# Rotary keys from one product, with the halves swapped by DMA

## The chip, the cores and the metric

One Trainium2 chip; the program runs on one of its cores. The metric is the device time of one execution in microseconds (us); lower is better. The time given is a median over executions.

## What is computed

A cross attention block is followed by a routed feed forward block, for 8 batches of 512 tokens and 512 context rows, model width 1024. The part that the change touches is the rotary share of the attention scores:

```
kv_c   = kv @ W_kvc                          # 512 x 256
k_rope = _rope(kv_c @ W_kr)                  # 512 x 64, one for all 16 heads
q_rope = _rope((q_c @ W_qr) per head)        # 512 x 64 per head
_rope(x) = [x1*cos - x2*sin, x1*sin + x2*cos]   # x1, x2: halves of 32
scores = (q_nope . k_nope + q_rope . k_rope) / sqrt(192)
```

## The kernel before, in words

Each engine has its own program, written out by hand; semaphores join them. In every product each float32 operand is split into a high part (fp32r) and a low part (the rest), and three of the four cross products are summed: high by high, high by low, low by high. ScalarE (ACT) makes the high part from the PSUM bank, VectorE (DVE) or GpSimd (POOL) the low part. The split weights are written to DRAM in the first batch and reloaded in the later ones. SyncE (SP) issues nearly all DMAs, one after another in a fixed order, and a wait on that queue holds all that stand behind it.

A batch is one run through 16 heads in 4 quads of 4. Each head has 4 score tiles of 128 queries by 512 keys (`scores`, five products of 512 columns into psS: k_hi by q_hi, k_hi by q_lo, the rotary stack by k_rope_hi and by k_rope_lo, k_lo by q_hi). Between them TensorE (PE) makes the next head's queries (`queries`, 9 products into psA) and keys (`keys`, 6 into psB), the values, the turned probabilities, the attention output and the output projection.

Between two batches (`body`, end, and `into_heads`) PE does the down projections of queries and context, then `rope_keys`, `queries(b, 0, 0)`, `keys(b, 0, 0)`, the last piece of the last batch's output projection (`out_end`, only when there was a batch before), and the first score tile. `rope_keys` (L1837) is 12 products: 6 with W_kr into psA and 6 with W_kr whose column halves are exchanged and signed into psB, each with its 64 columns written twice so that all 128 partitions are filled. VectorE's `rope_k` (L1250) multiplies psA by the cosines into `rope_term`, psB by the sines into `k_rope_term`, and adds them (L1261). ScalarE's `k_rope_hi` (L1020) and GpSimd's `k_rope_lo` (L746) make the two parts `krh` and `krl`, which the first score tile waits for.

The rotary queries of a quad are made by `rope_q`, and SP spreads them over the stack (`stack_head`, L469): per head four DMAs of 32 partitions by 512 elements. In the first batch all four heads' are issued in a row (`into`, L502), later only the first head's before the feed forward's loads (`ffn_loads`), the others behind.

## Time and profile before

| | |
|---|---|
| median of 3 executions | 3238.69 us (3235.26 to 3240.01) |
| the profiled execution's own time | 3238.15 us |
| its span in the trace | 3236.4 us |
| TensorE matmul busy | 3069.6 us, 95% of the span |
| VectorE busy | 2083.3 us, 64% |
| ScalarE busy | 1490.6 us, 46% |
| GpSimd busy | 714.7 us, 22% |
| mean granted TensorE clock | 0.977 |

Times in the trace are microseconds from the start of the span; a batch takes some 381 of them, and 1.75 us of the profiled execution lie outside the span. A row of the timeline gives an instruction's start and its duration; the start of the next one on the engine, not the duration, tells how fast a run of them goes. "Idle" in brackets is the time for which the engine had nothing, and what ended it.

### The profile page before, as it was taken

Reading aid. Unit: us, or ns where it says so; the run is one execution under the profiler, and the core shown is the slowest. Engines: PE = TensorE matmul, PEld = TensorE weight load, DVE = VectorE, ACT = ScalarE, POOL = GpSimd, SP = SyncE. Lnnn points to the kernel's source line nnn. Section 1 sums busy time; section 2 is a strip of 40 time slices with the busy share of each in tenths; the row PEclk is TensorE's granted clock in tenths of the full one; section 3 lists DMA queues with packets and bytes.
Section 4 is the critical chain, followed back from the end, with each engine's and each line's share of the span. In section 5 each row is a group of like instructions: output and inputs, shape, how many; then the busy total and the mean of one; then the engine's idle time right before and its main releaser. Section 6 shows DMA issues by size and latency. Waiting matters only on the chain.

```text
span 3236.4 us, 39942 instructions
## 1 busy us (share of the span) xinstructions
PE 3069.6 (95%) x13890; PEld 2386.5 (74%) x13890; DVE 2083.3 (64%) x4440; ACT 1490.6 (46%) x2907; POOL 714.7 (22%) x516
## 2 busy tenths in 40 slices
PE   7999999999999999999999999999999999999924
PEld 4788768887788867888678876888678876888722
DVE  2555537775577746777377764777467763777687
ACT  2655525553445435445264543555345452555411
POOL 5222241112211131110411113111311113111046
PEclk9999999999999999999999999999999999999955
DMA  6554444444534445433454444444454444544301
GB/s 205 195 172 160 173 163 164 136 140 148 192 121 140 140 156 189 134 128 130 156 193 140 140 146 172 141 140 140 141 181 140 140 131 150 186 140 137 118 27 4
DMA packets 170054, 473.34 MB, mean 146 GB/s; under 512 B 33136, under 2 KB 61424, under 8 KB 149248
## 3 DMA queue, kind: packets, MB, share of 16 engines
q1 hardware_dynamic: 164784, 469.91, 43.7%
q0 software_dynamic: 5072, 0.88, 0.6%
q8 instruction: 114, 1.87, 0.2%
q14 instruction: 84, 0.69, 0.1%
HBM read 369.84 MB, written 67.31 MB: 135 GB/s over the span
## 4 chain that ended last, share of the span: by engine, by line
PE 83%; DVE 7%; issue 4%; ACT 3%; POOL 2%; DMA 1%; SPq 0%; DVEq 0%; ACTq 0%; POOLq 0%
PE psC L1934 18%; PE psD L1927 10%; PE psA L1864 8%; PE psT L1916 6%; PE psA L1833 5%; PE psB L1873 5%; PE psD L1884 4%; PE psS L1901 3%; PE psB L1833 3%; PE psS L1907 3%; PE psS L1903 3%; PE psS L1902 3%; PE psS L1904 3%; PE psA L1855 2%; PE psB L1855 2%
## 5 line engine op out<-in xcount | busy, mean ns | idle before, releaser
L1934 PE MATMUL psC<-w_o_pair,attn_hi 128*128 128x512 f32 x1920 | 638.4, 413 | 18.7 <-DVE acc L1342 10.8
L1033 ACT ACTIVATE exps_ring<-exps_ring,neg_max 128x512 f32<-128x512 f32 x512 | 370.8, 724 | 424.9 <-DVE neg_max L1314 424.9
L1314 DVE CUSTOM_DVE_ANT_0 exps_ring<-psS,mask 128x512 f32<-128x512 f32 x512 | 353.2, 690 | 294.4 <-PE psS L1907 289.1
L1044 ACT ACTIVATE probsT_hi<-psT 128x512 fp32r<-128x512 f32 x512 | 305.8, 599 | 364.9 <-PE psT L1916 363.3
L1934 PEld LDWEIGHTS psC<-w_o_pair,attn_hi 128*128 128x128 f32 x1920 | 332.2, 189 | 89.5 <-DVE acc L1342 24.9
L1039 ACT ACTIVATE exps_ring<-exps_ring,row_sum_inverse 128x512 f32<-128x512 f32 x512 | 369.6, 722 | 61.0 <-DVE row_sum_inverse L1320 61.0
L1326 DVE TENSOR_TENSOR probsT_lo<-psT,probsT_hi 128x512 fp32r<-128x512 f32 x512 | 350.6, 686 | 58.3 <-ACT probsT_hi L1044 56.6
L1934 PE MATMUL psC<-w_o_pair,attn_lo 128*128 128x512 f32 x960 | 379.4, 395 | 0.0
L1342 DVE TENSOR_TENSOR acc<-acc,psC 128x512 f32<-128x512 f32 x448 | 303.2, 677 | 17.3 <-PE psC L1934 11.4
L1916 PE MATMUL psT<-ident,exps_ring 128*128 128x128 f32 x2048 | 305.0, 272 | 0.0
L1916 PEld LDWEIGHTS psT<-ident,exps_ring 128*128 128x128 f32 x2048 | 252.8, 139 | 66.4 <-issue 2.1
L1864 PE MATMUL psA<-q_c_hi,w_uq_ring 128*128 128x512 f32 x768 | 258.5, 391 | 0.1
L1934 PEld LDWEIGHTS psC<-w_o_pair,attn_lo 128*128 128x128 f32 x960 | 180.7, 188 | 42.2
L1901 PE MATMUL psS<-k_hi,q_hi 128*128 128x512 f32 x512 | 203.2, 397 | 6.0 <-DVE q_lo L1291 4.9
L1907 PE MATMUL psS<-k_lo,q_hi 128*128 128x512 f32 x512 | 200.4, 391 | 0.0
L1903 PE MATMUL psS<-k_rope_hi,q_rope_stack 128*128 128x512 f32 x512 | 199.7, 390 | 0.0
L1902 PE MATMUL psS<-k_hi,q_lo 128*128 128x512 f32 x512 | 199.7, 390 | 0.0
L1927 PE MATMUL psD<-probsT_hi,values_lo 128*128 128x512 f32 x512 | 199.5, 390 | 0.0
L1904 PE MATMUL psS<-k_rope_lo,q_rope_stack 128*128 128x512 f32 x512 | 199.4, 390 | 0.0
L1927 PE MATMUL psD<-probsT_hi,values_hi 128*128 128x512 f32 x512 | 199.2, 389 | 0.0
L1927 PE MATMUL psD<-probsT_lo,values_hi 128*128 128x512 f32 x512 | 199.2, 389 | 0.0
L1873 PE MATMUL psB<-kv_c_hi,w_uk_ring 128*128 128x512 f32 x512 | 180.3, 393 | 0.0
(301 smaller groups left out, 5497.8 us busy)
## 6 DMA issues: line engine op xcount, KB each, us to landing
w_o_pair<-w_o_split SPq DMA_DIRECT2D x112, 1024.0 KB, 5.4
w_uq_ring<-w_uq_split SPq DMA_DIRECT2D x114, 384.0 KB, 3.5
w_uv_quad<-w_uv_split SPq DMA_DIRECT2D x29, 1024.0 KB, 5.0
w_uk_ring<-w_uk_split SPq DMA_DIRECT2D x114, 256.0 KB, 2.8
w_qr_sorted<-w_qr_split SPq DMA_DIRECT2D x29, 768.0 KB, 4.3
x_stage<-in_x_dram SPq DMA_DIRECT2D x32, 512.0 KB, 5.9
x_stage<-in_ctx_dram SPq DMA_DIRECT2D x32, 512.0 KB, 4.1
acc<-in_x_dram SPq DMA_DIRECT2D x32, 512.0 KB, 5.3
```

What stands on the lines that cost most here:

```text
L1033: act.activation(E[:, qt, :], E[:, qt, :], ACT.Exp, scale=-1.0, bias=mx[:, i % 2, qt:qt + 1], accum_out=rs[:, i % 2, qt:qt + 1]).then_inc( ...
L1039: act.activation(E[:, qt, :], E[:, qt, :], ACT.Copy, scale=ri[:, i % 2, qt:qt + 1]).then_inc(s_prob, 1)
L1044: act.activation(PT[0][:, :, qt * P:(qt + 1) * P], psT[qt % 2][:, :].rearrange("p (c n) -> p c n", c=TT), ACT.Copy)\
L1314: dve.tensor_tensor_reduce(E[:, qt, :], psS[qt % 2][:, :], mask[:, qt, :], -SCALE, BIG, ALU.add, ALU.min, mx[:, i % 2, qt:qt + 1]).then_in ...
L1326: dve.tensor_tensor(PT[1][:, :, qt * P:(qt + 1) * P], psT[qt % 2][:, :].rearrange("p (c n) -> p c n", c=TT), hi.bitcast(F32), ALU.subtract ...
L1342: dve.tensor_tensor(a, a, psC[:, :], ALU.add).then_inc(freeC, 1)
L1864: mm_ = pe.matmul(psA[:, :], wuq[:, i % 2, s, c, :], qc[a][:, c, :], start=c + s + a == 0, stop=c == QB - 1 and s == 1)
L1873: mm_ = pe.matmul(psB[:, :], wuk[:, i % 2, s, c, :], kvc[a][:, c, :], start=c + s + a == 0, stop=c == CB - 1 and s == 1)
L1901: pe.matmul(ps, qh[:, cols], kh[:, :], start=True, stop=False)
L1916: mm_ = pe.transpose(psT[qt % 2][:, c * P:(c + 1) * P], E[:, qt, c * P:(c + 1) * P], ident)
L1927: mm_ = pe.matmul(psD[:, :], V[v][:, kt, i * P:(i + 1) * P], PT[p][:, kt, :], start=kt == 0 and v + p == 0, stop=kt == TT - 1 and v == 1)
L1934: mm_ = pe.matmul(ps[:, :], attn[a][:, 2 * pair + i, t * P:(t + 1) * P], WO[:, half, o, i, :], start=i + a + o == 0, stop=i + a == 2)
```

## The change

It touches one stage, between the down projection of the context and the first score tile of a batch, and the setup of W_kr:

- W_kr's columns are laid out once as 128: the 64 plain ones, then the 64 exchanged and signed ones. `rope_keys` is 6 products into psB alone; A0, the first position in psA's count, goes from 4 to 3.
- VectorE multiplies partitions 0 to 63 of psB by the cosines and 64 to 127 by the sines, both into `rope_term`. SP copies each half of it to the other half of `k_rope_term` (two DMAs, new function `swap_halves`, new semaphore), and VectorE adds the two. The sum stands behind `q_lo`.
- On ScalarE the high part of the first queries now stands ahead of `k_rope_hi`, that of the first keys behind it as before.
- In every score tile k_lo by q_hi is now third and the two rotary products last; in the first tile of a batch the waits for `krh` and `krl` stand directly before them.
- In SP's order `swap_halves` stands behind all four heads' stack loads in the first batch, and behind the first head's in the others, ahead of the feed forward's loads.
- The split W_kr that is stored and reloaded is half as large.

```diff
+            def swap_halves(b):
+                sp.wait_ge(freeB, b * BN + 4)
+                sp.dma_start(rk[0:R, :], rt[R:P, :]).then_inc(s_swap, 16)
+                sp.dma_start(rk[R:P, :], rt[0:R, :]).then_inc(s_swap, 16)
+
             def into(b, q, nxt, between=None):
...
                 if b == 0:
                     for i in range(HQ):
                         stack_head(b, q, i)
+                    if q == 0:
+                        swap_halves(b)
                     return
                 load_qr(b, q, nxt)
                 stack_head(b, q, 0)
+                if q == 0:
+                    swap_halves(b)
                 ffn_loads(b, q)
                 if between is not None:
                     between()
...
             def kr_hi():
-                act.wait_ge(s_setv, 4)
-                for w in range(2):
-                    act.activation(wkrs[:, w, 0], wkrr[:, w], ACT.Copy).then_inc(s_seta, 1)
+                act.wait_ge(s_setv, 2)
+                act.activation(wkrs[:, 0], wkrr, ACT.Copy).then_inc(s_seta, 1)
 
...
                 down(psB, fullB, b * BN + 2, kvc[0][:, 0, :], s_kvchi)
                 down(psA, fullA, b * AN + 3, kvc[0][:, 1, :], s_kvchi)
+                q_hi(b, 0, 0)
                 k_rope_hi(b)
-                q_hi(b, 0, 0)
                 k_hi(b, 0, 0)
...
-            def rope_k(b):
+            def rope_k_terms(b):
 
                 dve.wait_ge(s_rope, b * NR + 4)
                 dve.wait_ge(s_rhi, b * (NQ + 1) + 1)
                 dve.wait_ge(s_rlo, b * (NQ + 1) + 1)
-                dve.wait_ge(fullA, b * AN + 5)
-                dve.tensor_tensor(rt[:, :], psA[:, :], cosT[:, :], ALU.mult).then_inc(freeA, 1)
                 dve.wait_ge(fullB, b * BN + 4)
-                dve.tensor_tensor(rk[:, :], psB[:, :], sinT[:, :], ALU.mult).then_inc(freeB, 1)
-                dve.wait_ge(freeA, b * AN + 5)
+                dve.tensor_tensor(rt[0:R, :], psB[0:R, :], cosT[0:R, :], ALU.mult)
+                dve.tensor_tensor(rt[R:P, :], psB[R:P, :], sinT[R:P, :], ALU.mult).then_inc(freeB, 1)
+
+            def rope_k_sum(b):
                 dve.wait_ge(freeB, b * BN + 4)
+                dve.wait_ge(s_swap, 32 * (b + 1))
                 dve.tensor_tensor(rt[:, :], rt[:, :], rk[:, :], ALU.add).then_inc(s_rope, 1)
 
             def rope_q(b, q):
@@ -1456,8 +1466,9 @@
                 kvc_lo(b, 1, psA, freeA)
                 if ends is not None:
...
-                rope_k(b)
+                rope_k_terms(b)
                 q_lo(b, 0, 0)
+                rope_k_sum(b)
                 k_lo(b, 0, 0)
...
-            for a in range(2):
-                dve.tensor_copy(wkrr[:, 0, :, a, :], wkr).then_inc(s_setv, 1)
-            for a in range(2):
-                dve.tensor_scalar(wkrr[:, 1, :, a, 0:HR], wkr[:, :, HR:R], -1.0, None, ALU.mult)
-                ins = dve.tensor_copy(wkrr[:, 1, :, a, HR:R], wkr[:, :, 0:HR])
-            ins.then_inc(s_setv, 1)
-            for w in range(2):
-                dve.wait_ge(s_seta, 2 + w)
-                dve.tensor_tensor(wkrs[:, w, 1], wkrr[:, w], wkrs[:, w, 0].bitcast(F32), ALU.subtract)\
-                   .then_inc(s_wkrd, 8)
+            dve.tensor_copy(wkrr[:, :, 0, :], wkr)
+            dve.tensor_scalar(wkrr[:, :, 1, 0:HR], wkr[:, :, HR:R], -1.0, None, ALU.mult)
+            dve.tensor_copy(wkrr[:, :, 1, HR:R], wkr[:, :, 0:HR]).then_inc(s_setv, 1)
+            dve.wait_ge(s_seta, 2)
+            dve.tensor_tensor(wkrs[:, 1], wkrr, wkrs[:, 0].bitcast(F32), ALU.subtract).then_inc(s_wkrd, 16)
...
             def rope_keys(b):
                 pe.wait_ge(s_wkrd, 16 * (b + 1))
-                for ps, full, free, n, w in ((psA, fullA, freeA, b * AN + 4, 0),
-                                             (psB, fullB, freeB, b * BN + 3, 1)):
-                    wait_free(free, n)
-                    for c in range(CB):
-                        for s, a in ((0, 0), (0, 1), (1, 0)):
-                            mm_ = pe.matmul(ps[:, :], wkrs[:, w, s, c].rearrange("p a r -> p (a r)"), kvc[a][:, c, :],
-                                            start=c + s + a == 0, stop=c == CB - 1 and s == 1)
-                    mm_.then_inc(full, 1)
+                for c in range(CB):
+                    for s, a in ((0, 0), (0, 1), (1, 0)):
+                        mm_ = pe.matmul(psB[:, :], wkrs[:, s, c].rearrange("p w r -> p (w r)"), kvc[a][:, c, :],
+                                        start=c + s + a == 0, stop=c == CB - 1 and s == 1)
+                mm_.then_inc(fullB, 1)
 
             def rope_queries(b, q):
...
-                    if i == 0 and q == 0:
-                        pe.wait_ge(s_rhi, b * (NQ + 1) + 2)
-                        pe.wait_ge(s_rlo, b * (NQ + 1) + 2)
                 if not (very_first and qt < 2):
                     pe.wait_ge(s_sm, n - 1)
                 cols = slice(qt * P, (qt + 1) * P)
                 ps = psS[qt % 2][:, :]
                 pe.matmul(ps, qh[:, cols], kh[:, :], start=True, stop=False)
                 pe.matmul(ps, ql[:, cols], kh[:, :], start=False, stop=False)
-                pe.matmul(ps, stack[:, i, cols], krh[:, :], start=False, stop=False)
-                pe.matmul(ps, stack[:, i, cols], krl[:, :], start=False, stop=False)
                 if qt == 0:
                     pe.wait_ge(freeB, pos_b(b, q, 1 + i) + 1)
-                pe.matmul(ps, qh[:, cols], kl[:, :], start=False, stop=True).then_inc(s_S, 1)
+                pe.matmul(ps, qh[:, cols], kl[:, :], start=False, stop=False)
+                if qt == 0 and i == 0 and q == 0:
+                    pe.wait_ge(s_rhi, b * (NQ + 1) + 2)
+                pe.matmul(ps, stack[:, i, cols], krh[:, :], start=False, stop=False)
+                if qt == 0 and i == 0 and q == 0:
+                    pe.wait_ge(s_rlo, b * (NQ + 1) + 2)
+                pe.matmul(ps, stack[:, i, cols], krl[:, :], start=False, stop=True).then_inc(s_S, 1)
 
             def turn_probs(b, q, i, qt):
 
```

On the SP queue, in the first batch: the last stack loads and what follows them. Before:

```order
34 L479 DMA q_rope_stack<-rope_out 32x512 x2
35 L479 DMA q_rope_stack<-rope_hi 32x512 [waits rope_lo_done,rope_hi_done]
36 L479 DMA q_rope_stack<-rope_hi 32x512
37 L479 DMA q_rope_stack<-rope_out 32x512 x2
38 L373 DMA xT<-in_L_xattn_W_uq_dram 128x3x128 [waits fullB,fullA]
39 L377 DMA xT<-in_L_xattn_W_uk_dram 128x2x128
```

and with the change:

```order
34 L480 DMA q_rope_stack<-rope_out 32x512 x2
35 L480 DMA q_rope_stack<-rope_hi 32x512 [waits rope_lo_done,rope_hi_done]
36 L480 DMA q_rope_stack<-rope_hi 32x512
37 L480 DMA q_rope_stack<-rope_out 32x512 x2
38 L505 DMA k_rope_term<-rope_term 64x512 [waits freeB]
39 L506 DMA k_rope_term<-rope_term 64x512
40 L374 DMA xT<-in_L_xattn_W_uq_dram 128x3x128 [waits fullB,fullA]
41 L378 DMA xT<-in_L_xattn_W_uk_dram 128x2x128
```

The two copies stand behind the sixteen stack loads (four for each of four heads) and ahead of the raw weights of the coming heads.

VectorE at the same place, from the low part of the context to the first score tile's mask (`kv_c_lo` is the low part of the down projection). Before:

```order
39 L1247 TENSOR_TENSOR kv_c_lo<-psA,kv_c_hi 128x512 [waits kv_c_hi_done]
40 L1256 TENSOR_TENSOR rope_term<-psA,cosT 128x512 [waits rope_lo_done,fullA,rope_hi_done,rope_steps]
41 L1258 TENSOR_TENSOR k_rope_term<-psB,sinT 128x512 [waits fullB]
42 L1261 TENSOR_TENSOR rope_term<-rope_term,k_rope_term 128x512 [waits freeB,freeA]
43 L1291 TENSOR_TENSOR q_lo<-psA,q_hi 128x512 [waits q_hi_done]
44 L1296 TENSOR_TENSOR k_lo<-psB,k_hi 128x512 [waits k_hi_done]
45 L1314 ISA exps_ring,neg_max<-psS,mask 128x512 [waits scores,mask_steps]
```

and with the change:

```order
36 L1256 TENSOR_TENSOR kv_c_lo<-psA,kv_c_hi 128x512 [waits kv_c_hi_done]
37 L1265 TENSOR_TENSOR rope_term<-psB,cosT 64x512 [waits rope_lo_done,fullB,rope_hi_done,rope_steps]
38 L1266 TENSOR_TENSOR rope_term<-psB,sinT 64x512
39 L1301 TENSOR_TENSOR q_lo<-psA,q_hi 128x512 [waits q_hi_done]
40 L1271 TENSOR_TENSOR rope_term<-rope_term,k_rope_term 128x512 [waits k_rope_halves_swapped,freeB]
41 L1306 TENSOR_TENSOR k_lo<-psB,k_hi 128x512 [waits k_hi_done]
42 L1324 ISA exps_ring,neg_max<-psS,mask 128x512 [waits scores,mask_steps]
```

The sum has moved behind `q_lo` and waits for the copies; `k_lo` stands behind the sum.

ScalarE at the same place, before:

```order
24 L959 ACTIVATE kv_c_hi<-psB 128x512 [waits fullB]
25 L959 ACTIVATE kv_c_hi<-psA 128x512 [waits fullA]
26 L1022 ACTIVATE k_rope_hi<-rope_term 128x512 [waits rope_steps]
27 L1008 ACTIVATE q_hi<-psA 128x512 [waits fullA]
28 L1012 ACTIVATE k_hi<-psB 128x512 [waits fullB]
```

and with the change:

```order
23 L969 ACTIVATE kv_c_hi<-psB 128x512 [waits fullB]
24 L969 ACTIVATE kv_c_hi<-psA 128x512 [waits fullA]
25 L1017 ACTIVATE q_hi<-psA 128x512 [waits fullA]
26 L1031 ACTIVATE k_rope_hi<-rope_term 128x512 [waits rope_steps]
27 L1021 ACTIVATE k_hi<-psB 128x512 [waits fullB]
```

`q_hi` has moved ahead of `k_rope_hi`; `k_hi` still stands behind it.

## Rows read from the trace of the kernel before

**Rows 1.** The page: the span, and TensorE's busy time and instructions.

```profile
span 3236.4 us, 39942 instructions
...
PE 3069.6 (95%) x13890; PEld 2386.5 (74%) x13890; DVE 2083.3 (64%) x4440; ACT 1490.6 (46%) x2907; POOL 714.7 (22%) x516
```

**Rows 2.** The timeline of PE at the last change of batches: start, duration, instruction.

```profile
2745.79 0.47 PE L1844 MATMUL psA<-kv_c_hi,w_kr 128*128 128x512 f32 x1
...
2753.35 0.39 PE L1901 MATMUL psS<-k_hi,q_hi 128*128 128x512 f32 x1
...
2754.48 0.39 PE L1864 MATMUL psA<-q_c_hi,w_uq_ring 128*128 128x512 f32 x1
```

**Rows 3.** The timeline of DVE at the same place.

```profile
2747.53 0.69 DVE L1256 TENSOR_TENSOR rope_term<-psA,cosT 128x512 f32<-128x512 f32 x1 [1.15 <-PE psA L1844]
...
2749.58 0.69 DVE L1261 TENSOR_TENSOR rope_term<-rope_term,k_rope_term 128x512 f32<-128x512 f32 x1
2751.46 0.69 DVE L1291 TENSOR_TENSOR q_lo<-psA,q_hi 128x512 fp32r<-128x512 f32 x1 [1.18 <-ACT q_hi L1008]
...
2756.48 1.27 DVE L1359 BATCH_NORM_STATS2 ffn_stats<-xT 128x6 f32<-128x512 f32 x2
```

**Rows 4.** The timeline of ACT at the same place.

```profile
2750.31 0.63 ACT L1022 ACTIVATE k_rope_hi<-rope_term 128x512 fp32r<-128x512 f32 x1 [5.39 <-DVE rope_term L1261]
2750.85 0.58 ACT L1008 ACTIVATE q_hi<-psA 128x512 fp32r<-128x512 f32 x1
```

**Rows 5.** The timeline of POOL at the same place.

```profile
2751.02 1.29 POOL L748 TENSOR_TENSOR k_rope_lo<-rope_term,k_rope_hi 128x512 fp32r<-128x512 f32 x1 [17.72 <-ACT k_rope_hi L1022]
```

**Rows 6.** The timeline of SP's queue at the same place: the feed forward's first load.

```profile
2744.31 0.35 SPq L490 DMA_DIRECT2D xT<-out_dram  x1
```

**Rows 7.** Line L479 from 73 to 84 us: sixteen stack loads.

```profile
DMA to landing us min/median/max: 2.0/2.0/3.4
```

**Rows 8.** Line L490, all of its seven loads.

```profile
DMA to landing us min/median/max: 3.6/3.6/3.7
```

**Rows 9.** The timeline of DVE, second head: two operations back to back.

```profile
2764.78 0.69 DVE L1291 TENSOR_TENSOR q_lo<-psA,q_hi 128x512 fp32r<-128x512 f32 x1
2765.39 0.68 DVE L1296 TENSOR_TENSOR k_lo<-psB,k_hi 128x512 fp32r<-128x512 f32 x1
```

**Rows 10.** The timeline of PE, second head of the last batch.

```profile
2765.52 0.50 PE L1901 MATMUL psS<-k_hi,q_hi 128*128 128x512 f32 x1 [0.41 <-DVE q_lo L1291]
```

**Rows 11.** The timeline of SP's queue in the first batch.

```profile
82.57 1.23 SPq L479 DMA_DIRECT2D q_rope_stack<-rope_out  x2
83.89 0.53 SPq L373 DMA_DIRECT2D xT<-in_L_xattn_W_uq_dram  x1
```

**Rows 12.** The timeline of PE in the first batch.

```profile
70.86 0.47 PE L1844 MATMUL psA<-kv_c_hi,w_kr 128*128 128x512 f32 x1 [1.51 <-DVE kv_c_lo L1247]
...
79.62 0.40 PE L1864 MATMUL psA<-q_c_hi,w_uq_ring 128*128 128x512 f32 x1
...
91.66 0.50 PE L1901 MATMUL psS<-k_hi,q_hi 128*128 128x512 f32 x1 [1.40 <-DVE q_lo L1291]
```

**Rows 13.** The timeline of ACT in the first batch.

```profile
86.67 0.52 ACT L968 ACTIVATE w_uq_ring<-xT 128x384 fp32r<-128x384 f32 x1 [2.11 <-DMA xT<-in_L_xattn_W_uq_dram]
```

**Rows 14.** The timeline of PE: its two longest waits between the batches and near the end.

```profile
400.38 1.61 PE L1822 MATMUL psS<-ident,x_stage 128*128 128x128 f32 x8 [3.42 <-DVE x_stage L1238]
...
3083.78 1.22 PE L1934 MATMUL psC<-w_o_pair,attn_hi 128*128 128x512 f32 x2 [2.48 <-DVE acc L1627]
```

**Rows 15.** Windows: stretch, busy us of PE, PEld, DVE, ACT, POOL; granted clock; DMA share; GB/s.

```profile
70.80:74.00 3.20, 3.02 (x13) 2.24 (x13) 0.81 (x2) 0.00 (x0) 2.13 (x1) 1.00 0.00 0
401.00:404.00 3.00, 3.00 (x11) 2.52 (x10) 0.00 (x0) 1.19 (x2) 0.00 (x0) 0.50 0.88 296
3083.80:3087.00 3.20, 3.20 (x8) 2.52 (x9) 3.16 (x4) 0.00 (x0) 0.00 (x0) 0.50 0.00 0
```

**Rows 16.** Windows: the first batch from its first score tiles to its end.

```profile
80.00:445.00 365.00, 355.13 (x1645) 281.04 (x1644) 198.92 (x427) 200.51 (x394) 115.09 (x82) 1.00 0.51 172
```

More of the change, by code:

```diff
@@ L42, in xattn_ffn_kernel @@
     assert T == HALF and HQ * HR == P and 2 * R == P and D == 2 * HALF and NT * SLICE == D
-    A0, AQ = 4, 1 + HQ
+    A0, AQ = 3, 1 + HQ
     B0, BQ = 3, 1 + HQ
@@ L111, in xattn_ffn_kernel @@
             wDkv = sb_under("w_kvc", [P, DB, KVC])
-            wkrs = sb_under("w_kr", [P, 2, 2, CB, 2, R], F32R)
+            wkrs = sb_under("w_kr", [P, 2, CB, 2, R], F32R)
             rk = sb_under("k_rope_term", [P, T])
@@ L190, in xattn_ffn_kernel @@
         gb_end = xs[:, 1, :]
-        wkrt = wkrs[:, :, :, :, :, :].rearrange("p w s c a r -> p (w s c a r)")
+        wkrt = wkrs[:, :, :, :, :].rearrange("p s c w r -> p (s c w r)")
         wkr = acc[:, 1, 0:CB * R].rearrange("p (c r) -> p c r", c=CB)
-        wkrr = acc[:, 1, HALF:HALF + 4 * CB * R].rearrange("p (w c a r) -> p w c a r", w=2, c=CB, a=2)
+        wkrr = acc[:, 1, HALF:HALF + 2 * CB * R].rearrange("p (c w r) -> p c w r", c=CB, w=2)
         uq_raw0 = E[:, 0:2, 0:QB * P].rearrange("p s (c n) -> p s c n", c=QB)
@@ L238, in xattn_ffn_kernel @@
         s_krs = sem("w_kr_out")
+        s_swap = sem("k_rope_halves_swapped")
         s_gam = sem("gamma_in")
@@ L297, in xattn_ffn_kernel @@
         wo_dram = nc.dram_tensor("w_o_split", [PAIRS, 2, P, 4 * HALF], F32).ap()
-        kr_dram = nc.dram_tensor("w_kr_split", [P, 8 * CB * R], F32).ap()
+        kr_dram = nc.dram_tensor("w_kr_split", [P, 4 * CB * R], F32).ap()
         ss_dram = nc.dram_tensor("slope_sign_scratch", [NT, SLICE], F32).ap()
```

## The prediction

> **What bounds the kernel now.** I read the page first: TensorE is busy for 3069.6 us of a span of 3236.4 [rows 1], so the time is TensorE's order of work plus its waits. Then the timeline of the place that the change touches, in the last batch. TensorE starts the first rotary key product at 2745.79, the first score tile at 2753.35 and the work behind that tile at 2754.48, with no wait between [rows 2]: 33 products in 7.56 us, 0.229 each, and 5 more in 1.13 us. I call 2745.79 zero; the tile begins at 7.56 and the next work at 8.69. The other engines do the rotary keys beside this and are done in time: the sum of the terms starts at 2749.58 [rows 3], its high part at 2750.31 [rows 4], its low part at 2751.02 with 1.29 us [rows 5], ready at 2752.31, a microsecond before the tile. So the products are what costs time here, and the chain behind them is covered by 21 products. The change takes away 6 products and lengthens that chain by a trip through the DMA queue. The question is which of the two ends last.
>
> **Removed: 6 products in each of 8 batches.** 6 x 0.229 = 1.37 us a batch, 11.0 in all, if nothing else is late. TensorE would then reach the first tile at 6.19. VectorE has one bank less to read, and the first queries no longer wait for VectorE to free psA.
>
> **Added: the chain through the copies, batches 2 to 8.** Step by step from zero:
> - The 6 products into psB end where those into psA end now, so the first term starts at 1.74, as L1256 does at 2747.53 [rows 3].
> - Two operations on 64 partitions each. I take 0.69 us each, that of 128 partitions, since the elements per partition are the same. The second starts 0.61 after the first if it goes as two independent ones do now (2764.78 and 2765.39 [rows 9]), or up to 0.73 later if it waits for its end. I take 0.67; the terms are done at 3.10. The Trainium skill, "VectorE: DVE Perf Modes", section "Two Vector instructions with no wait between them", says that an instruction which starts in another quarter of the partitions than the one ahead starts only when all earlier ones have finished. That speaks for 0.73 here, and by it the sum below would be 0.5 us higher over 8 batches; no row here shows such a pair.
> - SP is idle then: it issued the feed forward's first load at 2744.31 [rows 6], and that one now stands behind the copies. It issues the first copy 0.03 later, at 3.13, and the second 0.61 behind it, as two stack loads take 1.23 us [rows 11]: 3.74.
> - Landing. No row has a copy of 64 partitions between the two halves. Nearest are the stack loads, 32 partitions each: 2.0 us in the median, 3.4 at most [rows 7]. Nothing in a copy excludes 2.0, and nothing is shorter in those rows. I take 2.2, a little over the quiet one because it carries twice the bytes and the loads that were under way here now come later. It lands at 5.94, and the sum starts at 5.97.
> - From the sum's start: the high part 0.73 later (2749.58 to 2750.31), the next operation of ScalarE 0.54 behind it [rows 4], which is k_hi now, since k_hi stands behind k_rope_hi; VectorE's low part starts 0.61 after it (2750.85 to 2751.46 [rows 3]) and takes 0.69; TensorE takes it 0.05 later (q_lo ends at 2765.47, the product starts at 2765.52 [rows 9, 10]). That is 2.62, so k_lo by q_hi starts at 8.59. Three products of 0.227 follow, and the next work starts at 9.27.
> - The low part of the rotary keys on GpSimd is ready 0.73 + 0.71 + 1.29 = 2.73 after the sum's start [rows 3 to 5]; its product comes at 3.07. It costs nothing; its cover is k_lo and two products, 0.34 us.
>
> Against 8.69 before, that is **+0.58 us a batch**, 4.1 for seven. The saved 1.37 us are spent as a wait of about 1.7 us before the tile, and what was expected to be hidden is not, above all because k_hi, needed by the tile's first product, queues behind the rotary high part on ScalarE. Moving the rotary products last does not help when the first product waits for the same chain. Break even is a landing of 1.6 us.
>
> **The first batch.** SP issues sixteen stack loads in a row there; the last two start at 82.57 and the next DMA at 83.89 [rows 11]. The copies stand behind them, while their terms have long been ready. First copy 83.89, second 84.50, landed 86.70, sum 86.73, next work behind the tile 3.30 later: 90.03. Before it was 79.62 [rows 12]: **+10.4 us**. Two corrections. TensorE waits for 1.40 us at 91.66 [rows 12], where the second head of the last batch waits for 0.41 [rows 10]; the excess comes from ScalarE, which stood until 86.67 for raw weights [rows 13]. With everything else ten microseconds later these weights are in time: -1.0. And TensorE is idle for more than 12 us (from about 76 to 88.7). After idle times of 3.42 and 2.48 us [rows 14] the granted clock was 0.50, the lower of the two levels, 1.2 GHz, in the stretches 401 to 404 and 3083.8 to 3087 [rows 15]. 3.2 us at half clock lose 1.6 us of work: +1.6, up to twice that. First batch: **+11.0**.
>
> **What is moved.** The feed forward's first two loads start at 2744.31 now [rows 6] and would start at about 4.4 after zero, 2750.2; 3.6 us [rows 8] make 2753.8, and VectorE uses the first at 2756.48 [rows 3]. Hidden by 2.7 us. Without that cover each microsecond would hold VectorE ahead of the second tile's mask. The two extra issues, 1.2 us, also push back the raw weights of the first batch; they are hidden by the ten microseconds above. The stack loads of the later heads stand behind the last store of the batch as before.
>
> **The order in every tile.** k_lo by q_hi is third, so k_lo must be there two products after the tile's start. In the second head k_lo ends at 2766.07 [rows 9] and the tile starts at 2765.52 [rows 10]; the product after a wait takes 0.50 instead of 0.39, so the third is due at about 2766.09. I take 0.03 us for two such heads a batch, 0.5 in all, between 0 and 0.14 each. Other tiles have the same five products: 0. The shorter setup of W_kr and its smaller reload lie beside long down projections: 0.
>
> **Sum.** 4.1 + 11.0 + 0.5 = +15.6 us on the profiled execution's 3238.15: **3253.8 us**. The median of the runs is 3238.69, so the profiled execution stands for them.
>
> **Rivals.**
> - *The clock falls in the later batches too.* The wait before the tile, 1.7 us and another 0.2 before the third product, lies between an idle time of 1.51 us, after which the clock was 1.00 [rows 12, 15], and one of 2.48, after which it was 0.50 [rows 14, 15]. If it falls each time, 1.6 us are lost seven times: +11.2, **3265 us**. The Trainium skill, "TensorE: Matmul & The Clock Gate", part 1, calls the lower clock the default that activity lifts; the two falls above agree, and by that rule alone this rival could come true in some batches and not in others. Chance 0.15.
> - *The copies land late.* At 3.1 to 3.4 us, as some stack loads do [rows 7], each batch loses 0.9 to 1.2 more, 8 to 9 in all: **3262 us**. Against it: no load is under way at this point any more. Chance 0.13.
> - *The first batch absorbs its delay.* The mechanism: the waits of that batch are set by chains of DMAs and split weights on SP and GpSimd that do not pass through the delayed tile. TensorE is idle for 9.9 of the 365 us from 80 to 445 [rows 16], 3.42 of them at 400.38 [rows 14]. If all of that were such, 1.1 of 11.0 us would be left, and the time would be 3238.15 + 1.1 + 4.6 = **3243.9 us**, no change within 0.2%. It decides from 9.1 us absorbed. Against it: SP's loads in that batch wait for TensorE's progress head by head. Chance 0.05.
> - *The saving comes through.* Only if the copies land 0.2 us after their issue, a tenth of the shortest stack load, would all 1.37 us be saved in seven batches, 9.6, against 9.5 in the first and its order: **3238 us**. Chance 0.02.
>
> **How the numbers follow.** The forecast's own case has 0.65. With a landing of 2.0 us, the pair at 0.61, half the clock's loss and no cost of the order it gives 3238.15 + 7 x 0.32 + 10.0 = 3250.4; with a landing of 2.5 and a clock loss of 3.2 it gives 3257.8. The range reaches to late copies and to the clock falling in every batch on one side, and below the own case on the other for a part absorbed: 3247 to 3266. 0.2% of the time, 6.5 us, is about what a measurement of this kernel can tell from no change, so the bound is 3245.2 on the median. Slower: 0.65 + 0.15 + 0.13 = 0.93, less a little, 0.92; within the bound: 0.06; faster: 0.02.
>
> **What would show it.** In the trace after: 6 products fewer a batch; in batches 2 to 8 a wait of 1.5 to 1.9 us before the first tile, released by k_hi, and the copies landing 2.0 to 2.5 us after their issue; the work behind the first tile 9.1 to 9.5 us after the first rotary key product. In the first batch a wait of 12 to 13 us that ends near 89 us, with a granted clock of 0.50 behind it, and everything later shifted by some 11 us. It is wrong if the copies land so early that no wait stands before the tile, or if the time from the first batch's end to the last one's is not longer than before.

## The result, and the profile after

| | before | after |
|---|---|---|
| median | 3237.57 us (3235.26 to 3240.01, 4 runs) | 3256.61 us (3254.73 to 3258.33, 4 runs) |
| the profiled execution, its span | 3238.15, 3236.4 us | 3256.62, 3254.5 us |
| TensorE matmul busy | 3069.6 us | 3066.2 us |
| mean granted TensorE clock | 0.977 | 0.975 |

The ratio is 1.0059, with a 95% interval from 1.0041 to 1.0076: slower. The medians lie 19.0 us apart, the profiled executions 18.5, and 15.6 were forecast. The page has 48 products fewer than [rows 1], six a batch:

```profile
span 3254.5 us, 39840 instructions
...
PE 3066.2 (94%) x13842; PEld 2373.1 (73%) x13842; DVE 2080.7 (64%) x4436; ACT 1491.9 (46%) x2906; POOL 715.4 (22%) x516
```

The timeline of PE, last batch, which answers to [rows 2]. The first rotary key product is zero again:

```profile
2764.46 0.50 PE L1847 MATMUL psB<-kv_c_hi,w_kr 128*128 128x512 f32 x1
...
2772.54 0.47 PE L1901 MATMUL psS<-k_hi,q_hi 128*128 128x512 f32 x1 [1.67 <-issue]
...
2773.22 0.50 PE L1905 MATMUL psS<-k_lo,q_hi 128*128 128x512 f32 x1
...
2774.03 0.40 PE L1867 MATMUL psA<-q_c_hi,w_uq_ring 128*128 128x512 f32 x1
```

The tile starts at 8.08 (7.56 before) and the next work at 9.57 (8.69). There is now a wait of 1.67 us, whose releaser the row does not name; the rows of the other engines show it, DVE first, then ACT, then SP's queue:

```profile
2766.25 0.68 DVE L1265 TENSOR_TENSOR rope_term<-psB,cosT 64x512 f32<-64x512 f32 x1 [1.09 <-PE psB L1847]
2766.94 0.69 DVE L1266 TENSOR_TENSOR rope_term<-psB,sinT 64x512 f32<-64x512 f32 x1
...
2770.60 0.69 DVE L1271 TENSOR_TENSOR rope_term<-rope_term,k_rope_term 128x512 f32<-128x512 f32 x1 [1.09 <-DMA k_rope_term<-rope_term]
2772.47 0.69 DVE L1306 TENSOR_TENSOR k_lo<-psB,k_hi 128x512 fp32r<-128x512 f32 x1 [1.18 <-ACT k_hi L1021]
```

```profile
2771.32 0.63 ACT L1031 ACTIVATE k_rope_hi<-rope_term 128x512 fp32r<-128x512 f32 x1 [2.54 <-DVE rope_term L1271]
2771.86 0.58 ACT L1021 ACTIVATE k_hi<-psB 128x512 fp32r<-128x512 f32 x1
```

```profile
2767.66 0.50 SPq L505 DMA_DIRECT2D k_rope_term<-rope_term  x1
2768.20 0.60 SPq L506 DMA_DIRECT2D k_rope_term<-rope_term  x1
2768.91 0.52 SPq L491 DMA_DIRECT2D xT<-out_dram  x1
```

Terms done at 3.17, second copy issued at 3.74, sum at 6.14, k_hi done at 7.98, tile at 8.08. The first batch has the same chain behind the stack loads. Its rows on SP's queue and on PE answer to [rows 11, 12]:

```profile
82.33 0.59 SPq L505 DMA_DIRECT2D k_rope_term<-rope_term  x1
82.97 0.60 SPq L506 DMA_DIRECT2D k_rope_term<-rope_term  x1
```

```profile
69.83 0.50 PE L1847 MATMUL psB<-kv_c_hi,w_kr 128*128 128x512 f32 x1 [1.41 <-DVE kv_c_lo L1256]
...
87.31 0.77 PE L1901 MATMUL psS<-k_hi,q_hi 128*128 128x512 f32 x1 [11.85 <-ACT k_hi L1021]
...
89.58 0.63 PE L1867 MATMUL psA<-q_c_hi,w_uq_ring 128*128 128x512 f32 x1
```

Two stretches behind waits, in the columns of [rows 15], both at the lower clock. The second is in the fifth batch, the only later one in which the clock fell behind the wait before the first tile:

```profile
87.20:91.00 3.80, 3.69 (x9) 2.91 (x10) 1.39 (x3) 0.34 (x2) 0.87 (x1) 0.50 0.79 269
...
1624.60:1627.80 3.20, 3.18 (x8) 2.47 (x9) 1.80 (x3) 0.00 (x0) 0.79 (x1) 0.51 0.56 219
```

Put together from the two traces, with the start of the first rotary key product of a batch as the mark ("next" is the work behind the first score tile):

| | before | after | difference |
|---|---|---|---|
| mark of batch 1 | 70.86 | 69.83 | -1.0 |
| mark of batch 1 to mark of batch 2 | 387.44 | 397.07 | +9.6 |
| batches 2 to 7, mark to mark | 2287.49 | 2297.56 | +10.1 |
| of it, mark to "next", batches 2 to 7 | 8.70 to 8.74 each | 9.62, 9.93, 9.56, 11.64, 9.61, 9.93 | +8.0 |
| last mark to the end | 490.61 | 490.04 | -0.6 |

### The profile page after: what moved, and what is told of

It reads as the page before. It is cut to its first block, busy times and chain, and to the rows that moved or that the text cites. A ratio compares the mean times of both kernels' runs of the same rounds, so it can differ in the third digit from the quotient of the medians.

```text
span 3254.5 us, 39840 instructions
## 1 busy us (share of the span) xinstructions
PE 3066.2 (94%) x13842; PEld 2373.1 (73%) x13842; DVE 2080.7 (64%) x4436; ACT 1491.9 (46%) x2906; POOL 715.4 (22%) x516
## 4 chain that ended last, share of the span: by engine, by line
PE 81%; DVE 7%; issue 4%; ACT 3%; POOL 3%; DMA 1%; SPq 0%; DVEq 0%; ACTq 0%; POOLq 0%
PE psC L1938 18%; PE psD L1931 10%; PE psA L1867 8%; PE psT L1920 6%; PE psB L1876 5%; PE psA L1839 4%; PE psD L1887 4%; PE psS L1905 4%; PE psS L1901 4%; PE psS L1911 3%; PE psS L1902 3%; PE psS L1908 3%; PE psB L1839 3%; PE psA L1858 2%; PE psB L1858 2%
```

## Experiments

Each was run beside the kernel before, and its ratio is against that. Four went together first (median of before 3237.38 us).

**1. The copies ahead in the first batch.** Is the first batch's delay SP's order?

```diff
-                    for i in range(HQ):
-                        stack_head(b, q, i)
+                    stack_head(b, q, 0)
                     if q == 0:
                         swap_halves(b)
+                    for i in range(1, HQ):
+                        stack_head(b, q, i)
                     return
```

> The changed kernel with one move: in the first batch SP issues the two copies of the halves behind the first head's four stack loads instead of behind all sixteen. Theory (the place on SP's queue makes the first batch's delay): the copies go out about 7.7 us earlier, TensorE's wait of 11.85 us before the first tile shrinks to about 4, still long enough for the granted clock to fall to 0.50, and the 1 us wait for raw weights may come back in part: 8 us less, about 3248.6. The later batches stay as they are. Rival (the delay is the landing and the chain behind it, not the place): no more than 1 us less, 3256.

Measured: 3250.36 us (3249.85 to 3255.18), ratio 1.0042 (1.0028 to 1.0056). SP's queue:

```profile
75.49 0.59 SPq L505 DMA_DIRECT2D k_rope_term<-rope_term  x1
76.12 0.60 SPq L506 DMA_DIRECT2D k_rope_term<-rope_term  x1
```

Issued seven microseconds earlier; the wait of 11.85 us is 4.25, and next comes at 12.81 instead of 19.75. Of these 6.9 us the medians show 6.3. So SP's order is the larger part of the first batch's loss, not all of it. The median lies 1.8 us above the expected 3248.6; the clock fell in the third batch here, behind a wait of 2.02 us, and that batch is 1.1 us longer than in the change's trace.

**2. The plain keys first.** The high part of the keys ahead of k_rope_hi on ScalarE, the low part ahead of the sum on VectorE. What does the order of the conversions cost?

```diff
                 q_hi(b, 0, 0)
-                k_rope_hi(b)
                 k_hi(b, 0, 0)
+                k_rope_hi(b)
...
                 q_lo(b, 0, 0)
-                rope_k_sum(b)
                 k_lo(b, 0, 0)
+                rope_k_sum(b)
```

> The changed kernel with the first keys' high part ahead of k_rope_hi on ScalarE, and their low part ahead of the sum on VectorE. Theory: the first three products of the tile then run at once, but the last one waits for the low part of the rotary keys on GpSimd (1.29 us, ready 2.73 us after the sum starts), so the work behind the tile moves only from 9.6 to about 9.25 us after the first rotary key product: 0.35 a batch, 3 us in all, 3253.6. Rival (ScalarE's order is the whole loss): the work behind the tile comes at 8.7 as before the change or earlier, 0.9 a batch, 3249 or less.

Measured: 3252.19 us (3251.09 to 3256.82), ratio 1.0045 (1.0032 to 1.0059). The tile starts at 6.26, so the saved products show there; next comes at 9.41. In the timeline of PE, last batch, the wait is inside the tile now:

```profile
2769.98 0.51 PE L1908 MATMUL psS<-k_rope_hi,q_rope_stack 128*128 128x512 f32 x1 [0.64 <-ACT k_rope_hi L1031]
2771.33 0.50 PE L1911 MATMUL psS<-k_rope_lo,q_rope_stack 128*128 128x512 f32 x1 [0.84 <-POOL k_rope_lo L758]
```

The order was worth only some 0.2 us in most batches: the copies and GpSimd's 1.28 us end the tile, whatever starts it. The medians lie 4.4 us apart, the profiled executions 0.8. In the traces "next" comes 3.7 us earlier over the seven later batches, 2.2 of it in the fifth, where the change had a late copy and a fallen clock (below). So the order is worth something between 1.4 us, seven times 0.2, and the 4.4 of the medians.

**3. No copies.** The sum adds `rope_term` to itself, so the rotary share of the scores is not the reference's. What do the copies cost?

```diff
             def swap_halves(b):
-                sp.wait_ge(freeB, b * BN + 4)
-                sp.dma_start(rk[0:R, :], rt[R:P, :]).then_inc(s_swap, 16)
-                sp.dma_start(rk[R:P, :], rt[0:R, :]).then_inc(s_swap, 16)
+                pass
...
-                dve.wait_ge(s_swap, 32 * (b + 1))
-                dve.tensor_tensor(rt[:, :], rt[:, :], rk[:, :], ALU.add).then_inc(s_rope, 1)
+                dve.tensor_tensor(rt[:, :], rt[:, :], rt[:, :], ALU.add).then_inc(s_rope, 1)
```

> The changed kernel with the two copies left out; the sum adds rope_term to itself, so the rotary share of the scores is not the reference's. It prices the copies: everything else of the change stays. Theory (the chain is long even without a copy, since the sum stands behind q_lo and k_hi behind the rotary high part): the work behind the first tile comes about 8.3 us after the first rotary key product, 0.4 less than before the change, not 1.37 less; the first batch loses nothing; the order of the products in each tile costs 0.3 a batch. Sum about 3236, level with the kernel before. Rival (the copies are all that stands against the saving): 11 us below the kernel before, less 2.4 for the order: 3229.

Measured: 3232.95 us (3231.58 to 3236.83, 11 runs), ratio 0.9987 (0.9978 to 0.9996), 3 us less than expected; next at 8.38 to 8.43. So the copies with their wait cost 23.7 us of the change (3256.61 to 3232.95), and without them 0.3 of the 1.37 us saved a batch arrives: k_hi still stands behind the sum and k_rope_hi.

**4. The order of products alone**, in the kernel before: k_lo by q_hi third, the rotary products last.

```diff
-                pe.matmul(ps, stack[:, i, cols], krh[:, :], start=False, stop=False)
-                pe.matmul(ps, stack[:, i, cols], krl[:, :], start=False, stop=False)
                 if qt == 0:
                     pe.wait_ge(freeB, pos_b(b, q, 1 + i) + 1)
-                pe.matmul(ps, qh[:, cols], kl[:, :], start=False, stop=True).then_inc(s_S, 1)
+                pe.matmul(ps, qh[:, cols], kl[:, :], start=False, stop=False)
+                pe.matmul(ps, stack[:, i, cols], krh[:, :], start=False, stop=False)
+                pe.matmul(ps, stack[:, i, cols], krl[:, :], start=False, stop=True).then_inc(s_S, 1)
```

> The kernel before with only the order of the products in each score tile changed: k_lo by q_hi third, the rotary products last. Theory: in the second and third head of a batch TensorE now stops for k_lo, and each stop costs 0.15 us, 0.04 of wait and 0.11 of a slower product behind it: 0.30 a batch, 2.4 us, 3240.0 against 3237.6. Rival (my prediction's 0.03 us each): 0.5 us in all, 3238.1. A third reading (the order costs nothing and the longer batches come from loads): 3237.6, and no third product of a tile longer than 0.40 us.

Measured: 3239.48 us (3237.81 to 3242.35, 11 runs), ratio 1.0005 (0.9996 to 1.0014): 2.1 us on the medians, which the interval does not separate from nothing. The timeline of PE shows the place, a second head:

```profile
1240.51 0.50 PE L1901 MATMUL psS<-k_hi,q_hi 128*128 128x512 f32 x1 [0.41 <-DVE q_lo L1291]
...
1241.11 0.50 PE L1905 MATMUL psS<-k_lo,q_hi 128*128 128x512 f32 x1
1241.44 0.40 PE L1906 MATMUL psS<-k_rope_hi,q_rope_stack 128*128 128x512 f32 x1
```

The third product takes 0.50 us and the fourth follows 0.33 behind it, instead of 0.23: k_lo is a little late, as argued, and the stop costs 0.04 for itself and 0.10 for the slower product behind it. The first tile of the second head takes 1.40 us instead of 1.26, that of the third 1.40 instead of 1.29. Later heads' first tiles are slower too (1.23 instead of 1.16 at the fifth), but the delay hardly grows behind the fourth head: the last one starts 0.1 to 0.4 us later than before in the seven later batches, counted from the mark.

The next three went together (median of before 3236.65 us).

**5. Edits 1 and 2 together**, with the new order of products in the first tile of a batch alone.

> The changed kernel with three things moved: the copies of the first batch behind the first head's stack loads, the first keys' parts ahead of the rotary ones on ScalarE and VectorE, and the order of the products as before the change in all tiles but the first of a batch. Theory: in the later batches the work behind the first tile comes at about 9.45 us as in keys_first, against 8.71 before the change, 0.75 us slower seven times; in the first batch it comes at about 81, a microsecond later than before the change; the order costs nothing any more. Sum about 3243.5. Rival (the parts share one cause and the second fix brings nothing on top of the first): 3249.

Measured: 3244.80 us (3243.52 to 3248.30), ratio 1.0026 (1.0017 to 1.0036); next at 11.99 in the first batch, 9.41 to 9.43 in the others but one (9.65). The gains nearly add up: 8.2 us are left of the 19.0 against the kernel before, so 10.9 come back. What is left stands at "next": 3.2 us in the first batch and 0.7 in each of the seven others (0.9 in one), where the tile waits for the copies and for GpSimd behind them.

**6. Edit 5, and 7. the kernel before, with the second head's query products ahead of the first tile.** Can nine products of other work, some 2 us, cover the wait?

```diff
+                    if head0:
+                        queries(b, quad, j)
                     scores(b, q, i, 0, vf)
...
-                    if quad is not None:
+                    if quad is not None and not head0:
                         queries(b, quad, j)
```

> both_moves with one more edit: in the first head of a batch TensorE makes the second head's queries (9 products, 2.05 us) ahead of the first score tile instead of behind it. Theory (what is missing is cover for the chain through the copies, and these products need nothing of it): TensorE comes to the rotary products at 8.9 us after the first rotary key product, when their low part is just ready, so the saved 6 products come through: 1.37 us less than before the change in seven batches, about 1 us less in the first. 3227, faster than both. Rival (the softmax chain behind the tile is now late by 0.7 us and the stop only moves to the first turned probabilities): about 3237, level with the kernel before.

> The kernel before with the same edit of TensorE's order alone (the second head's queries ahead of the first score tile of a batch). Theory: the tile waited for nothing there except 0.73 us in the first batch, so nothing but that comes back: 3236.7, no difference that can be measured. Rival (the order alone is what makes queries_ahead faster): as fast as queries_ahead, 3227 to 3230.

Measured: 3243.91 us (3240.56 to 3248.00), ratio 1.0022 (1.0013 to 1.0031), for edit 6; 3249.42 us (3246.76 to 3251.63), ratio 1.0040 (1.0026 to 1.0054), for edit 7, which was expected to change nothing. Neither theory held, and neither rival. The timeline of PE, second head of the fourth batch, of edit 6 and then of edit 7; [rows 10] has the place before:

```profile
1239.33 0.50 PE L1902 MATMUL psS<-k_hi,q_hi 128*128 128x512 f32 x1 [1.82 <-DVE q_lo L1302]
```

```profile
1243.54 0.49 PE L1901 MATMUL psS<-k_hi,q_hi 128*128 128x512 f32 x1 [1.85 <-DVE q_lo L1291]
```

The wait before the first tile is gone, and one of 1.8 us stands at the second head, where 0.41 stood. With edit 6 that tile starts 19.88 after the mark, before it was 19.73 [rows 2, 10]; with edit 7, where the first tile starts 2.0 later, it is 21.20. Counted from the end of the first tile, the second head's tile of the later batches comes after 10.4 us in edits 6 and 7, and after 11.0 to 11.1 in before, after and edit 5, whatever lies ahead (11.65 where the clock had fallen). So this stretch is paced by when the first tile ends, and not by the number of products on TensorE: nine products moved out of it (2.04 us) shorten it by 0.6 and leave the rest as a wait. Products saved ahead of the tile count as far as the tile ends earlier. The clock adds to it: behind waits of 1.82 us it fell in three batches of edit 6, and behind 1.83 and 1.85 us in two of edit 7.

**8. and 9. No DMA: VectorE writes across the halves.** In both, VectorE reads the sine half of psB at partitions 64 to 127 and writes its term to 0 to 63, where the cosine term is. Edit 8 sums on 64 partitions and has VectorE and GpSimd make the low parts of a half each. Edit 9 writes the sum twice, to either half, and makes the high and low parts as the change does:

```diff
-                dve.tensor_tensor(rt[0:R, :], psB[0:R, :], cosT[0:R, :], ALU.mult)
-                dve.tensor_tensor(rt[R:P, :], psB[R:P, :], sinT[R:P, :], ALU.mult).then_inc(freeB, 1)
+                dve.tensor_tensor(rk[0:R, :], psB[R:P, :], sinT[R:P, :], ALU.mult)
+                dve.tensor_tensor(rt[0:R, :], psB[0:R, :], cosT[0:R, :], ALU.mult).then_inc(freeB, 1)
...
-                dve.wait_ge(s_swap, 32 * (b + 1))
-                dve.tensor_tensor(rt[:, :], rt[:, :], rk[:, :], ALU.add).then_inc(s_rope, 1)
+                dve.tensor_tensor(rt[R:P, :], rt[0:R, :], rk[0:R, :], ALU.add)
+                dve.tensor_tensor(rt[0:R, :], rt[0:R, :], rk[0:R, :], ALU.add).then_inc(s_rope, 1)
```

The sum stands ahead of q_lo in both, and the new order of products is in the first tile of a batch alone, as in edit 5. So edit 9 differs from the change in three things, of which edit 4 priced the last at 2.1 us.

> One product for the rotary keys as in the change, but no copies: VectorE multiplies partitions 64 to 127 of the bank by the sines and writes the result to partitions 0 to 63, sums on 64 partitions, and ScalarE, VectorE and GpSimd write the high and low parts to both halves. First keys as before the change behind the rotary high part, other tiles in the order before the change. Theory (the saving was eaten by the trip through the DMA queue alone, because the softmax chain hangs on the end of the first tile): the sum starts 3.25 us after the first rotary key product instead of 6.14, the parts are there by 6.3, and the work behind the first tile comes at about 7.4 to 7.7 against 8.71 before the change; the whole chain behind moves with it. 1.0 to 1.3 us less in each of 8 batches and no half clock in the first: 3226 to 3229. Rival (the stop at the second head's first tile, 0.4 us before the change, takes the saving as it did in queries_ahead): 3236, level with the kernel before. Third (writes to other partitions are slow or held up): operations of over 1 us on 64 partitions and no gain.

Measured for edit 8: 3233.42 us (3230.91 to 3234.85, 11 runs) beside 3236.16, ratio 0.9991 (0.9982 to 1.0000); the tile starts at 6.26, next at 8.35, where 7.4 to 7.7 was expected. The timeline of DVE, POOL and PE says why:

```profile
1221.58 1.67 DVE L1273 TENSOR_TENSOR k_rope_lo<-rope_term,k_rope_hi 64x512 fp32r<-64x512 f32 x1
1223.28 0.69 DVE L1308 TENSOR_TENSOR k_lo<-psB,k_hi 128x512 fp32r<-128x512 f32 x1
```

```profile
1221.42 1.28 POOL L756 TENSOR_TENSOR k_rope_lo<-rope_term,k_rope_hi 64x512 fp32r<-64x512 f32 x1 [16.08 <-ACT k_rope_hi L1029]
```

```profile
1224.02 0.51 PE L1908 MATMUL psS<-k_lo,q_hi 128*128 128x512 f32 x1 [0.60 <-DVE k_lo L1308]
```

VectorE's half took 1.67 us beside GpSimd's, 1.67 to 1.75 in all seven later batches. In the first batch VectorE's started first, and GpSimd's took longer:

```profile
75.62 0.69 DVE L1273 TENSOR_TENSOR k_rope_lo<-rope_term,k_rope_hi 64x512 fp32r<-64x512 f32 x1
```

```profile
75.66 1.77 POOL L756 TENSOR_TENSOR k_rope_lo<-rope_term,k_rope_hi 64x512 fp32r<-64x512 f32 x1 [3.06 <-ACT k_rope_hi L1029]
```

Edit 9 takes VectorE's operation away:

> As lanes, but VectorE writes the sum to both halves (two operations on 64 partitions), and the high and low parts are made as in the change, one operation on ScalarE and one on GpSimd for all 128 partitions. In lanes VectorE's low part on 64 partitions took 1.67 us instead of 0.69 while GpSimd made the other half beside it, and k_lo stood behind it. Theory (that collision is what was left; the copies' trip was the rest): sum on both halves done 4.6 us after the first rotary key product, k_lo at 6.6, low part of the rotary keys at 6.7, and the work behind the first tile at about 7.4 against 8.71 before the change and 8.35 in lanes. The saving of 1.3 us a batch comes through to the second head, whose tile hangs on the first tile by the softmax chain: 3225.7, faster than the kernel before by 10.5. Rival (the second head's first tile, where TensorE already stopped for 0.4 us, is bound by work of VectorE and ScalarE that does not move with the first tile): half or less comes through, 3231.

Measured: 3226.76 us (3224.21 to 3227.33, 6 runs) beside 3237.14, ratio 0.9966 (0.9954 to 0.9978): faster than both kernels. The timeline of DVE, then of PE, last batch:

```profile
2736.25 0.69 DVE L1262 TENSOR_TENSOR k_rope_term<-psB,sinT 64x512 f32<-64x512 f32 x1 [1.11 <-PE psB L1844]
2736.95 0.68 DVE L1263 TENSOR_TENSOR rope_term<-psB,cosT 64x512 f32<-64x512 f32 x1
2737.67 0.68 DVE L1267 TENSOR_TENSOR rope_term<-rope_term,k_rope_term 64x512 f32<-64x512 f32 x1
2738.37 0.68 DVE L1268 TENSOR_TENSOR rope_term<-rope_term,k_rope_term 64x512 f32<-64x512 f32 x1
2738.97 0.68 DVE L1298 TENSOR_TENSOR q_lo<-psA,q_hi 128x512 fp32r<-128x512 f32 x1
```

```profile
2734.45 0.50 PE L1844 MATMUL psB<-kv_c_hi,w_kr 128*128 128x512 f32 x1
...
2740.71 0.39 PE L1898 MATMUL psS<-k_hi,q_hi 128*128 128x512 f32 x1
...
2741.87 0.39 PE L1864 MATMUL psA<-q_c_hi,w_uq_ring 128*128 128x512 f32 x1
...
2752.94 0.51 PE L1898 MATMUL psS<-k_hi,q_hi 128*128 128x512 f32 x1 [0.42 <-DVE q_lo L1298]
```

The terms are done at 3.18 and the sum at 4.60, where the change has it done at 6.83. The tile starts at 6.26 with no wait, next at 7.42, 1.27 us less than before, and the second head's tile at 18.49, 1.24 less than 19.73: the end of the first tile carries through. The eight batches' "next" come 9.6 us earlier in all, and the medians lie 10.4 apart. (The profiled spans lie 14.4 apart; the stretches of before at 401 and 3083.8 with the clock at 0.50 [rows 15] have none to answer to them in this run, and the clock stays at 1.00 until its closing stage.)

## Why the prediction was right, and where its terms were off

The sign, the mechanism and the time came as forecast: 3256.6 us against 3253.8, inside the 3250.4 to 3257.8 of the forecast's own case. Part of that agreement is luck: the first batch came 2.4 us below its term and everything behind it 4.9 above (9.5 instead of 4.6), one late copy and the fallen clock in the fifth batch among it. By the steps:

- **Six products saved, spent as a wait.** Right: a wait of 1.65 to 1.77 us in five of the seven later batches where 1.7 was said, 2.03 in one, 2.95 in one. Edit 9 shows that the saving was real, 1.27 of 1.37 us, and that it was the chain that took it.
- **The chain, +0.58 us a batch.** Mis-sized: +0.83 to +0.91 in four of seven batches. Terms done at 3.17 (said 3.10: the pair is 0.69 apart, not 0.67), second copy at 3.74 as said, sum at 6.14 (said 5.97: the copy lands after 2.3 us, not 2.2), and from there 2.62 to the product with k_lo, exactly as said. The last 0.13 lie behind it: that product takes 0.50, so three of them take 0.81 us, not 0.68. The prediction charged the wait for k_lo, and not the slower product that follows it. The queue behind ScalarE's rotary high part is there as described [rows 4].
- **Where the trace decides between rule and row.** The pair was priced between 0.61 and 0.73. It came at 0.69 to 0.70, as long as one operation takes, and in edit 9 so did the pair of sums, which differ in the output's half alone, while q_lo behind them followed after 0.60. So the second of such a pair does not overlap the first, as the Trainium skill, "VectorE: DVE Perf Modes", section "Two Vector instructions with no wait between them", has it.
- **Two batches at 9.93 and one at 11.64.** In the third batch the second copy landed 2.3 us after its issue, as elsewhere, but VectorE started the sum 0.45 us after the landing instead of 0.09; edit 1 has the same in its third batch. In the seventh the products ahead of the tile take 0.3 longer, with edits 2, 5 and 9 too. Nothing here tells why, in either. In the fifth batch the second copy landed 3.6 us after its issue, the late landing of one rival; the wait grew to 2.95 us and the clock fell behind it, the other rival (0.51, shown above). Together that cost 2.0 us. So each rival came true, in one batch of seven instead of all. Line L506 as a whole has this copy as an exception:

```profile
DMA to landing us min/median/max: 2.3/2.3/3.6
```

The DMA view of 1618 to 1623 us in the same trace has a transfer on another queue that no other batch has at this place, 16 KB of instructions:

```profile
q8 instruction: 1, 0.02, 1.9%
```

It began 0.55 us after the second copy's issue and took 1.5. That the two belong together is not shown; it is one batch.

- **The first batch, +11.0.** Too much: from the start of the trace to the second batch's mark it is +8.6. SP's order is the larger part of the cause, as said (edit 1). The copies go out at 82.33 and 82.97, where 83.89 and 84.50 were said: the first product starts 1.03 us earlier, and SP's queue is another 0.5 ahead. "Next" comes 9.96 us later in the trace (89.58 against 79.62), where 10.4 was said; 0.9 of it is the half clock already, which stretches the way from the sum to next from 3.30 to 4.21. The wait at 91.66 fell from 1.40 to 0.31 us, as said. The half clock lasted until about 92 us, some 2.4 us of work instead of 1.6.
- **"The shorter setup of W_kr and its smaller reload: 0".** The 1.03 us are not the setup: edits 4 and 7 keep the old one and have their first product at 69.91 and 70.01, edits 3, 8 and 9 have the new one and start it at 70.29 to 70.62. So the place of this mark differs by some 1 us between traces whatever the setup, and nothing here tells why. But the wait of 3.42 us at 400.38 is 2.45 after, and this 1 us is not a delay absorbed either: it is 2.45 to 2.49 in every run with the six products, edits 3, 8 and 9 included, where the first batch is not delayed, and 3.32 and 3.35 in edits 4 and 7. The load that it hangs on lands 5.7 us after its issue instead of 6.6. Something in the change saves that; what it is stays open: in before the first reload of W_kr is issued only at 411.7.
- **The order in the tile, 0.5.** Mis-sized: edit 4's medians have it at 2.1 us, with an interval that reaches from below nothing to 4.5, and its trace at 0.1 to 0.4 us a batch. A stop costs 0.14 us where 0.03 was said; the slower tiles of the later heads, for which 0 was said, add little. The six middle batches lose 2.1 us behind "next" in the table above, some 0.5 of it the half clock of the fifth.
- **The end.** Not foreseen: at 3083.78 before waited 2.48 us and ran at 0.50 behind it [rows 14, 15]; the same place in after waited 2.49, and the clock stayed at 1.00. From next to the end the last batch is 1.5 us shorter.

Sum of what was measured: 8.6 for the first batch, 8.0 + 0.9 for "next" in the seven others, 2.1 behind it in six, 1.5 less behind the last: 18.1, the difference of the spans.

Two rivals fell. The saving did not come through, because no copy landed in less than 2.2 us. The first batch absorbed little: it is 9.96 us late at "next" and 8.6 at the second mark, and the 1.1 us at 91.66 and the 1.0 at 400.38 lie between. What was called hidden was hidden: the feed forward's loads, which start 4.45 us behind the mark instead of 1.48 ahead of it [rows 2, 6], held nobody. VectorE uses the first at 2776.03 and has no wait for it.

Still open: what makes the clock fall. Within one kernel the length of the wait alone does not tell it (below).

## What to carry to other kernels

Work taken off the bounding engine counts only as far as the next thing that waits for the engine's *result* comes earlier; read how far ahead of its use the side chain is (1 us here) before a step of 3 us, a DMA and its issue (here from 3.17 to 6.14), goes into it. Halves of a tile that must be exchanged can be written by VectorE to the other partitions at the price of one more short operation, and the DMA is not needed. A queue in a fixed order delays a late, urgent copy by everything that stands before it, so look at each place of the program where the order differs, above all the first round.

## What the runs showed of the hardware

- VectorE reading partitions 64 to 127 of PSUM and writing 0 to 63 of SBUF takes 0.69 us for 512 float32, no more than in place, and from SBUF 0 to 63 to SBUF 64 to 127 it takes 0.68.
- VectorE's low part of the rotary keys, with both inputs in SBUF, stood still beside GpSimd's on the other half: 1.67 us instead of 0.69, ending 0.55 behind GpSimd's end. Where it started 0.04 us ahead of GpSimd's, it took 0.69 and GpSimd's 1.77 instead of 1.28. q_lo, which reads PSUM and SBUF, took 0.69 while GpSimd worked [rows 3, 5]. The Trainium skill, "GPSIMD Engine Reference", section "Specifications", says that the two contend when VectorE's instruction has two inputs in SBUF, and these traces agree. They do not show it beside every operation of GpSimd: beside the one that makes the mask from a single tensor (438.53 to 440.47 in before), VectorE's sum of two SBUF tensors at 439.43 took 0.69.
- A copy of 128 KB between the halves landed 2.2 to 2.4 us after its issue in seven batches of eight; in the other one the pair took 2.6 and 3.6.
- A product behind even a short stop takes 0.47 to 0.51 us instead of 0.39, and the next one follows some 0.1 later than usual.
- The clock fell after waits of 2.95 us (after), 2.02 (edit 1), 1.82 (edit 6, where it was 0.51 from 2004 to 2007.2 us) and 1.85 (edit 7, sixth batch, 0.51 from 2009.8 to 2013), and stayed at 1.00 after others of 1.85 (edit 7, fourth batch), 1.82 (edit 6, fourth batch), 2.03 and 2.49 (after). Two batches of edit 6 with such a fall are 382.7 us long from mark to mark, the four without one 381.1 to 381.8. So the same wait can cost over a microsecond beyond itself or nothing, and a forecast of it can only be a chance.
